# First image in another order, and the queries' weight loaded by the scalar engine's queue

## The chip, the cores and the metric

One core of one Trainium2 chip runs the kernel. The metric is the device time of one execution in microseconds, as a median over runs. The kernel before takes 1978.31 us (three runs, 1976.14 to 1979.01).

## What is computed

A self-attention block over 16 images of 512 channels and 32x32 positions, with a group norm ahead of it, four 512x512 weights and a residual, all in float32:

```python
residual = hidden_states
h = group_norm(hidden_states, norm_gamma, norm_beta)
q = conv1x1(h, wq, bq)
k = conv1x1(h, wk, bk)
v = conv1x1(h, wv, bv)
...
attn = jnp.einsum('bci,bcj->bij', qf, kf) * scale
attn = jax.nn.softmax(attn, axis=2)
out = jnp.einsum('bcj,bij->bci', vf, attn).reshape(B, C, H, W)
out = conv1x1(out, wo, bo)
return residual + out
```

## The kernel before

The program is written by hand, engine by engine: one block each for SyncE, GpSimd, TensorE, ScalarE and VectorE, with semaphores between them. What an engine does is the order of the lines of its block; nothing is scheduled for it. Image 0 is written out apart (`first=True`), the others run in a loop.

**Precision.** Every float32 factor is split in two: ScalarE makes a rounded high part (`*_hi`), VectorE subtracts it to get the rest (`*_lo`), and `product` (lines 418 to 421) makes three matmuls of them, high by high and the two mixed ones. So each factor costs a cast on ScalarE, then a subtraction on VectorE, and only then TensorE may use it.

**Setup, once.** The product of the weights of queries and keys is made first (lines 431 to 438, 48 matmuls, into banks 0 to 3); it takes the place of two of the projections. Twelve filler matmuls on zeros run ahead of it (line 428). Then `wo` is transposed by TensorE (line 444), a bias vector is summed by GpSimd and multiplied out in four one-column matmuls (lines 447 to 452), and the product of the transposed `wo` with `wv` is made (lines 453 to 462, 48 matmuls, banks 4 to 7). It waits for the low parts of `wo` (VectorE, line 989) and of `wv` (GpSimd, line 361). Meanwhile VectorE takes the group norm's statistics of image 0 (lines 895 to 933), GpSimd turns them into a scale and a shift per channel (lines 366 to 385), and ScalarE applies these to the image (`normalise`, line 642).

**The first image.** The product T of weight and image uses seven block products (a Strassen-like scheme) instead of eight. The blocks of the image are A11, A12, A22 and the sums S1 to S4, which VectorE makes (lines 945 to 957), ScalarE casts (line 651) and VectorE splits (line 964). `make_first_t` on TensorE (line 472) runs the seven products in `T_ORDER`, two halves r = 0, 1 for each, six matmuls of 512 columns a half. Three of them reuse a bank, so ScalarE copies the partial sum out before ("a", "b", "y", line 715). VectorE then adds up six blocks D3, D1, D2, B11, B22, B21 from banks and copies (`add_t`, lines 1022 to 1051), and each of these and D4 is cast (line 724) and split (`low_t`, line 1057).

**The scores.** `make_scores` (lines 516 to 555) takes the seven block products of T with the image in `S_ORDER`: product 7 for four column groups q, then product 1, and so on. Ahead of product 1 for q = 0 TensorE waits until B21 for r = 0 is added, since that addition reads the bank which product 1 overwrites:

```python
if p == 1:
    if q == 0:
        pe.wait_ge(t_split, t_count(b, first, 7, 0, L_AT[4]))
        pe.wait_ge(t_added, t_count(b, first, 6, 0, C_AT["B21"]))
```

After the scores come column maxima, exponentials, the values' product and the outputs, image by image; their code is not touched.

**Loads.** SyncE issues all loads of the start in one queue (lines 276 to 287): `wk` and `wq` in four pieces each by turns, `bq`, the image, `wo`, three vectors of 512 numbers (gamma, beta, `bo`), `wv`.

## Time and profile before

| | us |
|---|---|
| median of 3 runs | 1978.31 |
| the profiled execution | 1976.81 |
| its span, first to last instruction | 1974.8 |
| TensorE busy in the span | 1966.2 |
| VectorE busy | 1630.7 |
| ScalarE busy | 998.1 |
| GpSimd busy | 327.0 |

The mean granted clock of TensorE is 0.999 of full. Times in the rows below are counted from the start of the span. A row of the timeline begins with the start and the duration; instructions of one engine overlap by a little (the next one starts before the last has been acknowledged), so the distance from start to start is what one costs where an engine is busy throughout. In brackets stands the idle time before a row, and what ended it.

### The profile page before, as it was taken

Reading aid. Unit: us, or ns where it says so; the run is one execution under the profiler, and the core shown is the slowest. Engines: PE = TensorE matmul, PEld = TensorE weight load, DVE = VectorE, ACT = ScalarE, POOL = GpSimd, SP = SyncE. Lnnn points to the kernel's source line nnn. Section 1 sums busy time; section 2 is a strip of 40 time slices with the busy share of each in tenths; the row PEclk is TensorE's granted clock in tenths of the full one; section 3 lists DMA queues with packets and bytes.
Section 4 is the critical chain, followed back from the end, with each engine's and each line's share of the span. In section 5 each row is a group of like instructions: output and inputs, shape, how many; then the busy total and the mean of one; then the engine's idle time right before and its main releaser. Section 6 shows DMA issues by size and latency. Waiting matters only on the chain.

```text
span 1974.8 us, 29827 instructions
## 1 busy us (share of the span) xinstructions
PE 1966.2 (100%) x9924; PEld 1680.8 (85%) x9924; DVE 1630.7 (83%) x2285; ACT 998.1 (51%) x1528; POOL 327.0 (17%) x240
## 2 busy tenths in 40 slices
PE   9999999999999999999999999999999999999999
PEld 7888888888888888888888888888888888888887
DVE  8998896978969789696887969889698896978857
ACT  6474453645536464454644536446364553646443
POOL 2022120111202012020121201212011120212202
PEclk9999999999999999999999999999999999999999
DMA  7336252363414535054350533615236252363402
GB/s 250 128 150 171 76 148 96 149 170 127 114 77 155 164 149 139 31 173 146 149 159 32 173 125 149 170 66 151 102 149 170 108 124 87 150 169 149 92 31 43
DMA packets 55035, 254.66 MB, mean 129 GB/s; under 512 B 8160, under 2 KB 8160, under 8 KB 50400
## 3 DMA queue, kind: packets, MB, share of 16 engines
q1 hardware_dynamic: 36720, 221.01, 29.8%
q0 software_dynamic: 18288, 33.30, 10.8%
q8 instruction: 16, 0.26, 0.1%
q14 instruction: 11, 0.09, 0.0%
HBM read 213.39 MB, written 74.45 MB: 146 GB/s over the span
## 4 chain that ended last, share of the span: by engine, by line
PE 94%; DVE 0%; issue 0%; POOL 0%; ACT 0%; POOLq 0%
PE psum L419 32%; PE psum L420 31%; PE psum L421 31%; DVE red L1161 0%; DVE scores L1166 0%; POOL wide L394 0%; DVE scores L1152 0%; DVE scores L1351 0%; DVE scores L1220 0%; ACT room L730 0%; POOLq L393 0%; ACT scores L744 0%
## 5 line engine op out<-in xcount | busy, mean ns | idle before, releaser
L419 PE MATMUL psum<-big_hi 128*128 128x512 f32 x1056 | 412.0, 390 | 1.6 <-POOL big_lo L361 1.6
L420 PE MATMUL psum<-big_lo,big_hi 128*128 128x512 f32 x1056 | 411.6, 390 | 0.0
L421 PE MATMUL psum<-big_hi,big_lo 128*128 128x512 f32 x1056 | 411.4, 390 | 0.0
L419 PE MATMUL psum<-big_hi,h_hi 128*128 128x512 f32 x896 | 348.5, 389 | 0.0
L420 PE MATMUL psum<-big_lo,h_hi 128*128 128x512 f32 x896 | 348.5, 389 | 0.0
L421 PE MATMUL psum<-big_hi,h_lo 128*128 128x512 f32 x896 | 348.5, 389 | 0.0
L1152 DVE TENSOR_TENSOR scores<-psum,room 128x512 f32<-128x512 f32 x192 | 130.6, 689 | 199.6 <-ACT room L826 149.6
L826 ACT COPY room<-psum 128x512 f32<-128x512 f32 x192 | 113.1, 589 | 291.2 <-PE psum L421 291.2
L419 PE MATMUL psum<-w_split,h_hi 128*128 128x256 f32 x896 | 253.6, 283 | 0.3 <-ACT room L730 0.3
L420 PE MATMUL psum<-w_split,h_hi 128*128 128x256 f32 x896 | 253.6, 283 | 0.0
L421 PE MATMUL psum<-w_split,h_lo 128*128 128x256 f32 x896 | 253.6, 283 | 0.0
L419 PEld LDWEIGHTS psum<-big_hi 128*128 128x128 f32 x1056 | 198.8, 188 | 42.6 <-issue 1.7
L421 PEld LDWEIGHTS psum<-big_hi,big_lo 128*128 128x128 f32 x1056 | 198.6, 188 | 41.7
L420 PEld LDWEIGHTS psum<-big_lo,big_hi 128*128 128x128 f32 x1056 | 198.8, 188 | 40.6
L1173 DVE TENSOR_TENSOR big_lo<-scores,big_hi 128x512 fp32r<-128x512 f32 x256 | 197.2, 810 | 24.9 <-ACT big_hi L754 24.9
L420 PEld LDWEIGHTS psum<-big_lo,h_hi 128*128 128x128 f32 x896 | 168.2, 188 | 35.0
L421 PEld LDWEIGHTS psum<-big_hi,h_lo 128*128 128x128 f32 x896 | 168.2, 188 | 34.9
L419 PEld LDWEIGHTS psum<-big_hi,h_hi 128*128 128x128 f32 x896 | 168.2, 188 | 34.9
L394 POOL PARTITION_ALL_REDUCE wide<-red x32 | 56.9, 1828 | 841.2 <-DVE red L1161 841.2
L1166 DVE TENSOR_TENSOR scores<-scores,wide 128x1024 f32<-128x1024 f32 x128 | 162.8, 1322 | 32.8 <-POOL wide L394 32.8
L405 POOL PARTITION_ALL_REDUCE wide<-red x32 | 104.1, 3254 | 478.3 <-DVE red L1201 469.4
L419 PE MATMUL psum<-h_hi,w_split 128*128 128x512 f32 x448 | 174.5, 389 | 0.0
(134 smaller groups left out, 3445.3 us busy)
## 6 DMA issues: line engine op xcount, KB each, us to landing
w_split<-kept_t SPq DMA_DIRECT2D x15, 3584.0 KB, 11.8
w_split<-kept_v SPq DMA_DIRECT2D x15, 3584.0 KB, 11.3
room<-in_x SPq DMA_DIRECT2D x64, 512.0 KB, 3.5
out<-scores POOLq DMA_DIRECT2D x127, 256.0 KB, 6.8
room<-in_x SPq DMA_DIRECT2D x61, 256.0 KB, 5.7
red<-in_x SPq DMA_DIRECT2D x30, 256.0 KB, 3.7
wide<-in_x SPq DMA_DIRECT2D x30, 256.0 KB, 6.9
kept_t<-w_split SPq DMA_DIRECT2D x1, 3584.0 KB, 10.9
```

What stands on the lines that cost most here:

```text
L394: nc.gpsimd.partition_all_reduce(wide[:, half, :], red[:, half, :], P, MAX_ALL).then_inc(max_all, 1)
L405: nc.gpsimd.partition_all_reduce(wide[:, half, :], red[:, half, :], P, ADD_ALL).then_inc(sum_all, 1)
L419: nc.tensor.matmul(o, a_hi, b_hi, start=start, stop=False, skip_group_check=True)
L420: nc.tensor.matmul(o, a_hi, b_lo, start=False, stop=False, skip_group_check=True)
L421: return nc.tensor.matmul(o, a_lo, b_hi, start=False, stop=stop, skip_group_check=True)
L826: nc.scalar.copy(snap_s(q, n), bank[alpha_s[q % 2]][:]).then_inc(s_snapped, 1)
L1152: nc.vector.tensor_tensor(scores[:, o, :], bank[at][:], snap_s(q, n), ALU.add).then_inc(s_added, 1)
L1166: nc.vector.tensor_tensor(scores[:, j:j + 2, :], scores[:, j:j + 2, :], wide[:, half, :].unsqueeze(1).to_broadcast([P, 2, HALF]), ALU.subt ...
L1173: nc.vector.tensor_tensor(p_lo[:, j, :], scores[:, half * NJ + j, :], p_hi[:, j, :].bitcast(F32), ALU.subtract).then_inc(p_split, 1)
```

## The change

All of it lies in the setup and in image 0. The loads of `wq` go from SyncE's queue to ScalarE's, two before and two after the load of the table of functions; gamma, beta and `bo` go there too, gamma and beta behind the eight casts of `wk` and `wq`. On TensorE eight fillers stay of twelve; the bias matmuls go ahead of the transposes of `wo` and into another bank; the product with `wv` starts when its first pieces are split. VectorE, not GpSimd, splits the first piece of `wv`. Image 0 takes its blocks in another order (A12 and product 2 ahead of S1 and product 5), casts and splits A22 and A12 ahead of the splits of the weight, and interleaves the additions and splits of T differently. The code that all later images run is as before.

```diff
+T_FIRST = (4, 2, 5, 7, 6, 1, 3)
...
-H_FIRST = (A22, S1, A12, S3, S2, A11, S4)
+H_FIRST = (A22, A12, S1, S3, S2, A11, S4)
...
@@ sync
             for o in range(KC):
                 sp.dma_start(wk_raw[:, o, :], w_d["k"][:, o, :]).then_inc(wk_in[o], 16)
-                sp.dma_start(wq_raw[:, o, :], w_d["q"][:, o, :]).then_inc(wq_in[o], 16)
...
-            for n, a in enumerate(vec_d):
-                sp.dma_start(vecs[:, n, :], a, allow_slow_non_contiguous=True).then_inc(vec_in, 16)
@@ gpsimd
-            pool.wait_ge(vec_in, 16 * len(vec_d))
+            pool.wait_ge(scale_in, 32)
...
-            for o in range(KC):
+            for o in range(1, KC):
                 low_wv(o)
@@ tensor
-            for _ in range(12):
+            for _ in range(8):
...
             pe.wait_ge(consts_set, 4)
+            pe.wait_ge(bias_step, 2)
+            for c in range(KC):
+                mm = nc.tensor.matmul(bank[2 * KC - 1][:, c:c + 1], wide[:, 0, cols(c)], primer[:, 0:1],
+                                      start=True, stop=True, skip_group_check=True)
+            mm.then_inc(bias_summed, 1)
             for c in range(KC):
                 pe.wait_ge(wo_in[c], 16)
             for n in range(KC):
+                if n == KC - 1:
+                    pe.wait_ge(t_bias_set, 1)
...
                 if o == 0:
-                    pe.wait_ge(t_bias_set, 1)
-                pe.wait_ge(wot_split, KC if o == 0 else o + 1)
-                pe.wait_ge(wv_split, o + 1)
+                    pe.wait_ge(wv_first, 1)
+                else:
+                    pe.wait_ge(wv_split, o)
                 for c in range(KC):
+                    if o == 0:
+
+                        pe.wait_ge(wot_split, c + 1)
...
-                pe.wait_ge(wt_split, 7)
-                for p in T_ORDER:
+                pe.wait_ge(wt_split, 3)
+                for p in T_FIRST:
+                    pe.wait_ge(wt_split, W_AT[p])
@@ scalar
+            for o in range(2):
+                act.dma_start(wq_raw[:, o, :], w_d["q"][:, o, :]).then_inc(wq_in[o], 16)
             nc.scalar.preload_act_table(ACT.Exp)
+            for o in range(2, KC):
+                act.dma_start(wq_raw[:, o, :], w_d["q"][:, o, :]).then_inc(wq_in[o], 16)
...
+            for n in range(2):
+                act.dma_start(vecs[:, n, :], vec_d[n], allow_slow_non_contiguous=True).then_inc(scale_in, 16)
...
+            act.dma_start(vecs[:, 2, :], vec_d[2], allow_slow_non_contiguous=True).then_inc(vec_in, 16)
...
+            high_wot(0)
+            high_raw_wv(0)
+            for o in range(1, KC):
+                high_wot(o)
+            for o in range(1, KC):
+                high_raw_wv(o)
             for k in (2, 3):
                 normalise(0, k)
+            high_h(0, 0, True)
+            high_h(0, 1, True)
 
             act.wait_ge(wd_set, 4)
             for p in W_ORDER:
                 high_wt(p)
-            high_h(0, 0, True)
...
+                for r in range(2):
+                    snap(0, r, 0, "a", T_FIRST_AT[4], True)
                 high_h(0, 2, True)
-                high_h(0, 1, True)
                 copy_wov(0)
                 copy_wov(1)
                 high_h(0, 3, True)
-                for r in range(2):
-                    snap(0, r, 0, "a", T_AT[4], True)
@@ vector
+                if o == 0:
+                    dve.wait_ge(wv_high, 1)
+                    nc.vector.tensor_tensor(wvs_lo[:, 0, :], wv_raw[:, 0, :], wvs_hi[:, 0, :].bitcast(F32),
+                                            ALU.subtract).then_inc(wv_first, 1)
...
+            low_h(0, 0, True)
+            low_h(0, 1, True)
             for p in W_ORDER:
...
-            low_h(0, 0, True)
...
-                low_h(0, 1, True)
                 low_h(0, 2, True)
-
-                dve.wait_ge(bv_in, 16)
-                dve.wait_ge(vec_in, 16 * len(vec_d))
-                for c in (0, 1):
-                    row_dots(c)
                 low_h(0, 3, True)
                 sum_h(0, 2, True)
 
+                dve.wait_ge(bv_in, 16)
+                dve.wait_ge(vec_in, 16)
+                row_dots(0)
+                low_h(0, 4, True)
+                low_h(0, 5, True)
+                row_dots(1)
...
-                low_h(0, 6, True)
-                low_t(0, 0, "D3", True)
-                low_t(0, 1, "D3", True)
-                for name in C_ORDER[1:]:
-                    for r in range(2):
-                        add_t(0, r, name, True)
-                for name in L_ORDER[1:]:
-                    for r in range(2):
-                        low_t(0, r, name, True)
...
+                low_both("D3")
+                add_both("D1", "D2", "B11")
+                low_both("D4", "B11", "D2", "D1")
+                add_both("B22", "B21")
+                low_both("B22", "B21")
```

On VectorE, from the last split of a block of the image to the end of the splits of T (L964 is `low_h`, L1037 to L1050 are the additions D1, D2, B11, B22, B21, L1057 is `low_t`), before:

```order
L1057 TENSOR_TENSOR big_lo<-scores,big_hi 128x512 [waits t_high] x2
L1037 TENSOR_TENSOR scores<-psum,scores 128x512 [waits t_snapped,t_summed]
L1037 TENSOR_TENSOR scores<-psum,room 128x512 [waits t_snapped,t_summed]
L1041 SCALAR_TENSOR_TENSOR scores<-psum,t_bias,scores 128x512 [waits t_snapped,t_summed]
L1041 SCALAR_TENSOR_TENSOR scores<-psum,t_bias,room 128x512 [waits t_snapped,t_summed]
L1044 TENSOR_TENSOR scores<-scores 128x512 [waits t_added] x2
L1046 TENSOR_TENSOR scores<-scores 128x512 [waits t_added] x2
L1050 TENSOR_TENSOR scores<-psum,scores 128x512 [waits t_high] x2
L1057 TENSOR_TENSOR big_lo<-psum,big_hi 128x512 [waits t_high] x2
L1057 TENSOR_TENSOR big_lo<-scores,big_hi 128x512 [waits t_high] x10
L1234 TENSOR_TENSOR scores<-wide 128x512 [waits wov_copied,t_split]
```

And with the change, at the same place (L986 is `low_h`, L1062 to L1077 the additions, L1084 `low_t`):

```order
L1084 TENSOR_TENSOR big_lo<-scores,big_hi 128x512 [waits t_high] x2
L1064 TENSOR_TENSOR scores<-psum,scores 128x512 [waits t_snapped,t_summed]
L1064 TENSOR_TENSOR scores<-psum,room 128x512 [waits t_snapped,t_summed]
L1068 SCALAR_TENSOR_TENSOR scores<-psum,t_bias,scores 128x512 [waits t_snapped,t_summed]
L1068 SCALAR_TENSOR_TENSOR scores<-psum,t_bias,room 128x512 [waits t_snapped,t_summed]
L1071 TENSOR_TENSOR scores<-scores 128x512 [waits t_added] x2
L1084 TENSOR_TENSOR big_lo<-psum,big_hi 128x512 [waits t_high] x2
L1084 TENSOR_TENSOR big_lo<-scores,big_hi 128x512 [waits t_high] x6
L1073 TENSOR_TENSOR scores<-scores 128x512 [waits t_added] x2
L1077 TENSOR_TENSOR scores<-psum,scores 128x512 [waits t_high] x2
L1084 TENSOR_TENSOR big_lo<-scores,big_hi 128x512 [waits t_high] x4
```

The additions of B22 and B21 (L1073, L1077) now stand behind eight splits (L1084 x2 and x6) that stood behind them before.

On ScalarE, from the bias terms to the casts of the weight, before (L671 casts `wo`, L674 `wv`, L642 is `normalise`, L658 casts the weight, L651 a block of the image):

```order
L674 CAST big_hi<-scores 128x512 [waits wv_in3]
L642 ACTIVATE room<-room,h_shift,h_scale 128x1024 [waits scale_step] x2
L658 ACTIVATE w_split<-psum 128x512 [waits wkq_summed,wd_set]
L658 ACTIVATE w_split<-psum 128x512 [waits wkq_summed] x2
L658 ACTIVATE w_split<-scores 128x512 [waits wd_set] x4
L651 CAST h_hi<-room 128x1024 [waits h_full]
L642 ACTIVATE room<-room,h_shift,h_scale 128x1024 [waits scale_step] x2
L651 CAST h_hi<-room 128x1024 [waits h_full,bias_summed]
L651 CAST h_hi<-scores 128x1024 [waits h_summed]
L693 COPY wide<-psum 128x512 [waits wov_summed] x2
L651 CAST h_hi<-scores 128x1024 [waits h_summed]
```

With the change (L673 and L679 load the vectors, L688 casts `wo`, L692 `wv`, L653 is `normalise`, L669 casts the weight, L662 a block):

```order
L692 CAST big_hi<-scores 128x512 [waits wv_in3]
L653 ACTIVATE room<-room,h_shift,h_scale 128x1024 [waits scale_step] x2
L662 CAST h_hi<-room 128x1024 [waits h_full] x2
L669 ACTIVATE w_split<-psum 128x512 [waits wkq_summed,wd_set]
L669 ACTIVATE w_split<-psum 128x512 [waits wkq_summed] x2
L669 ACTIVATE w_split<-scores 128x512 [waits wd_set] x4
L653 ACTIVATE room<-room,h_shift,h_scale 128x1024 [waits scale_step] x2
L738 COPY scores<-psum 128x512 [waits t_summed,bias_summed]
L738 COPY room<-psum 128x512 [waits h_split,h_summed,t_summed]
L662 CAST h_hi<-red 128x1024 [waits h_summed]
L716 COPY wide<-psum 128x512 [waits wov_summed] x2
L662 CAST h_hi<-scores 128x1024 [waits h_summed]
```

Two loads stand ahead of the bias terms and one behind them, and the casts of two blocks stand ahead of those of the weight.

On TensorE, behind the first product of weights, before:

```order
L421 MATMUL psum<-big_hi,big_lo 128x512
L444 MATMUL psum<-ident,scores 128x128 [waits wo_in2,wo_in1,wo_in3,wo_in0,consts_set]
L444 MATMUL psum<-ident,scores 128x128 x15
L450 MATMUL psum<-primer,wide 128x1 [waits bias_step,wot_split]
L450 MATMUL psum<-primer,wide 128x1 x3
L419 MATMUL psum<-big_hi 128x512 [waits wv_split,wot_split,t_bias_set]
```

With the change (L444 is the bias, L453 the transpose, L420 opens the product with `wv`):

```order
L422 MATMUL psum<-big_hi,big_lo 128x512
L444 MATMUL psum<-primer,wide 128x1 [waits bias_step,consts_set]
L444 MATMUL psum<-primer,wide 128x1 x3
L453 MATMUL psum<-ident,scores 128x128 [waits wo_in2,wo_in3,wo_in1,wo_in0]
L453 MATMUL psum<-ident,scores 128x128 x11
L453 MATMUL psum<-ident,scores 128x128 [waits t_bias_set]
L453 MATMUL psum<-ident,scores 128x128 x3
L420 MATMUL psum<-big_hi 128x512 [waits wot_split,wv_first]
```

The bias matmuls, and with them the wait for GpSimd's sum (`bias_step`), have come ahead of the transposes.

## Rows read from the trace of the kernel before

**Rows 1.** The page, part 1: busy time, share of the span, instructions by engine.

```profile
PE 1966.2 (100%) x9924; PEld 1680.8 (85%) x9924; DVE 1630.7 (83%) x2285; ACT 998.1 (51%) x1528; POOL 327.0 (17%) x240
```

**Rows 2.** Timeline of TensorE, from the fillers to the first scores: start, duration, line.

```profile
1.58 5.49 PE L429 MATMUL psum<-h_hi 128*128 128x512 f32 x12 [1.58 <-DVE h_hi L967]
...
6.87 0.62 PE L419 MATMUL psum<-big_hi 128*128 128x512 f32 x1
...
19.06 1.94 PE L444 MATMUL psum<-ident,scores 128*128 128x128 f32 x16 [0.88 <-DMA scores<-in_wo]
...
23.79 0.47 PE L419 MATMUL psum<-big_hi 128*128 128x512 f32 x1 [1.65 <-POOL big_lo L361]
...
28.20 0.40 PE L419 MATMUL psum<-big_hi 128*128 128x512 f32 x1
...
36.38 0.39 PE L419 MATMUL psum<-h_hi,w_split 128*128 128x512 f32 x1
...
55.42 0.39 PE L419 MATMUL psum<-big_hi,h_hi 128*128 128x512 f32 x1
...
60.87 0.39 PE L419 MATMUL psum<-big_hi,h_hi 128*128 128x512 f32 x1
```

**Rows 3.** Chain that ended last, where image 0 goes from scores to values: start, duration.

```profile
92.79 0.60 DVE scores L1152
```

**Rows 4.** Timeline of VectorE in setup and image 0.

```profile
12.05 5.15 DVE L895 BATCH_NORM_STATS2 bn<-room 128x6 f32<-128x512 f32 x8 [0.84 <-DMA room<-in_x]
...
20.34 2.48 DVE L989 TENSOR_TENSOR big_lo<-psum,big_hi 128x512 fp32r<-128x512 f32 x4 [0.15 <-ACT big_hi L671]
...
27.67 0.69 DVE L1007 SCALAR_TENSOR_TENSOR w_split<-psum,w_split 128x512 fp32r<-128x512 f32 x1 [1.51 <-ACT w_split L658]
...
48.24 1.23 DVE L964 TENSOR_TENSOR h_lo<-red,h_hi 128x1024 fp32r<-128x1024 f32 x1
...
49.39 1.29 DVE L1057 TENSOR_TENSOR big_lo<-scores,big_hi 128x512 fp32r<-128x512 f32 x2
...
55.98 1.28 DVE L1050 TENSOR_TENSOR scores<-psum,scores 128x512 f32<-128x512 f32 x2
...
58.37 6.10 DVE L1057 TENSOR_TENSOR big_lo<-scores,big_hi 128x512 fp32r<-128x512 f32 x10
...
73.08 2.50 DVE L1225 TENSOR_TENSOR w_split<-scores,w_split 128x512 fp32r<-128x512 f32 x4 [2.48 <-ACT w_split L704]
```

**Rows 5.** Timeline of SyncE's issues of loads.

```profile
1.30 0.43 SPq L278 DMA_DIRECT2D scores<-in_wq  x1
...
10.73 2.20 SPq L285 DMA_DIRECT2D vecs<-in_beta  x1
```

**Rows 6.** Stretches: busy us by engine, granted clock, DMA share, GB/s.

```profile
5.00:5.50 0.50, 0.50 (x2) 0.40 (x2) 0.50 (x1) 0.00 (x0) 0.00 (x0) 1.00 0.70 135
...
14.00:14.50 0.50, 0.50 (x4) 0.42 (x3) 0.50 (x2) 0.00 (x0) 0.50 (x1) 1.00 1.10 451
...
17.50:18.00 0.50, 0.50 (x3) 0.22 (x2) 0.45 (x5) 0.00 (x0) 0.00 (x0) 1.00 1.32 130
...
24.00:26.00 2.00, 2.00 (x7) 1.52 (x7) 1.97 (x4) 2.00 (x2) 2.00 (x2) 0.60 0.03 8
```

**Rows 7.** Timeline of GpSimd in the setup.

```profile
15.92 1.29 POOL L376 TENSOR_TENSOR wide<-wide 128x512 f32<-128x512 f32 x1
...
22.37 5.01 POOL L361 TENSOR_TENSOR big_lo<-scores,big_hi 128x512 fp32r<-128x512 f32 x4
```

**Rows 8.** Timeline of ScalarE in setup and image 0.

```profile
10.79 1.34 ACT L664 ACTIVATE red<-scores,bq_s 128x512 f32<-128x512 f32 x2 [0.30 <-DMA bq_s<-in_bq]
...
19.72 2.05 ACT L671 CAST big_hi<-psum 128x512 fp32r<-128x512 f32 x4 [2.28 <-PE psum L444]
...
23.79 2.38 ACT L642 ACTIVATE room<-room,h_shift,h_scale 128x1024 f32<-128x1024 f32 x2
...
29.59 1.07 ACT L651 CAST h_hi<-room 128x1024 fp32r<-128x1024 f32 x1
```

More of the change, by code:

```diff
@@ L32 @@
 T_AT = {p: n + 1 for n, p in enumerate(T_ORDER)}
+T_FIRST = (4, 2, 5, 7, 6, 1, 3)
+T_FIRST_AT = {p: n + 1 for n, p in enumerate(T_FIRST)}
 W_ORDER = (2, 1, 3, 4, 5, 7, 6)
@@ L647, in high_h @@
                 if a in (A11, A12, A22):
-                    act.wait_ge(h_full, 2 if first and a == A22 else count(b, KC, KC))
+                    act.wait_ge(h_full, 2 if first and a in (A22, A12) else count(b, KC, KC))
                 else:
@@ L668, in _, with high_wot, high_raw_wv @@
             nc.scalar.copy(b12_copy, b12).then_inc(b12_copied, 1)
-            for o in range(KC):
+            act.wait_ge(bias_summed, 1)
+            nc.scalar.copy(t_bias[:], bank[2 * KC - 1][:, 0:KC]).then_inc(t_bias_set, 1)
+            def high_wot(o):
                 act.wait_ge(wo_turned, o + 1)
                 nc.scalar.copy(wot_hi[:, o, :], bank[KC + o]).then_inc(wot_high, 1)
-            for o in range(KC):
+            def high_raw_wv(o):
                 act.wait_ge(wv_in[o], 16)
                 nc.scalar.copy(wvs_hi[:, o, :], wv_raw[:, o, :]).then_inc(wv_high, 1)
-                if o == 0:
-                    act.wait_ge(bias_summed, 1)
-                    nc.scalar.copy(t_bias[:], bank[KC][:, 0:KC]).then_inc(t_bias_set, 1)
+            high_wot(0)
[4 more added lines that the diff above has]
+                high_raw_wv(o)
             for k in (2, 3):
                 normalise(0, k)
+            high_h(0, 0, True)
+            high_h(0, 1, True)
             act.wait_ge(wd_set, 4)
@@ L719, in high_t @@
                 if name == "D4":
-                    act.wait_ge(t_summed, t_count(b, first, 7, r, T_AT[3]))
+                    act.wait_ge(t_summed, t_count(b, first, 7, r, (T_FIRST_AT if first else T_AT)[3]))
                     nc.scalar.copy(t_hi[:, OF_T[p], r, :], bank[alpha_t[r]][:]).then_inc(t_high, 1)
@@ L948, in sum_h @@
                     dve.wait_ge(h_full, count(b, KC, KC))
-                    nc.vector.tensor_tensor(blocks[S1], a21, blocks[A22], ALU.add).then_inc(h_summed, 1)
+                    nc.vector.tensor_tensor(blocks_[S1], a21, blocks[A22], ALU.add).then_inc(h_summed, 1)
                 elif n == 1:
@@ L953, in sum_h @@
                     dve.wait_ge(h_summed, count(b, 4, 1))
-                    nc.vector.tensor_tensor(blocks[S2], blocks[S1], blocks[A11], ALU.subtract).then_inc(h_summed, 1)
+                    nc.vector.tensor_tensor(blocks[S2], blocks_[S1], blocks[A11], ALU.subtract).then_inc(h_summed, 1)
                 else:
@@ L1029, in add_t @@
                 if name == "D3":
-                    dve.wait_ge(t_summed, t_count(b, first, 7, r, T_AT[5]))
+                    dve.wait_ge(t_summed, t_count(b, first, 7, r, (T_FIRST_AT if first else T_AT)[5]))
                     dve.wait_ge(t_snapped, t_count(b, first, 3, r, 1))
@@ L1034, in add_t @@
                 elif name == "D1":
-                    dve.wait_ge(t_summed, t_count(b, first, 7, r, T_AT[7]))
+                    dve.wait_ge(t_summed, t_count(b, first, 7, r, (T_FIRST_AT if first else T_AT)[7]))
                     dve.wait_ge(t_snapped, t_count(b, first, 3, r, 3))
@@ L1038, in add_t @@
                 elif name == "D2":
-                    dve.wait_ge(t_summed, t_count(b, first, 7, r, T_AT[1]))
+                    dve.wait_ge(t_summed, t_count(b, first, 7, r, (T_FIRST_AT if first else T_AT)[1]))
                     dve.wait_ge(t_snapped, t_count(b, first, 3, r, 2))
@@ L1086, in make_first_t, with add_both, low_both @@
                     row_dots(c)
+                low_h(0, 6, True)
                 dve.wait_ge(bv_used, KC)
                 nc.vector.tensor_tensor(out_bias[:], wo_bv[:], bo_s, ALU.add).then_inc(biases_set, 1)
-                low_h(0, 6, True)
-                low_t(0, 0, "D3", True)
-                low_t(0, 1, "D3", True)
-                for name in C_ORDER[1:]:
-                    for r in range(2):
-                        add_t(0, r, name, True)
-                for name in L_ORDER[1:]:
-                    for r in range(2):
-                        low_t(0, r, name, True)
+                def add_both(*names):
+                    for name in names:
+                        for r in range(2):
+                            add_t(0, r, name, True)
+                def low_both(*names):
+                    for name in names:
+                        for r in range(2):
+                            low_t(0, r, name, True)
+                low_both("D3")
[3 more added lines that the diff above has]
+                low_both("B22", "B21")
             def left(b, n):
```

25 lines of the change are left out of this document (9 added, 16 removed).

## The prediction

> **What bounds the kernel now.** First the page's busy times [rows 1]: TensorE works 1966.2 of 1974.8 us, so only its idle and slow stretches, 8.6 us in all, can be won, and whatever makes it wait is paid in full. The change touches the setup and image 0 alone, so the timeline of TensorE up to the first scores [rows 2] comes next. The reader is to see there three losses: the fillers and the wait up to 6.87, where the first product begins; 0.88 us ahead of the transposes at 19.06, for the load of `wo`; and 1.65 us ahead of the product with `wv` at 23.79, for GpSimd's split. That product then runs slowly at first: its opening twelve matmuls last from 23.79 to 28.20, 4.41 us, where a half of T (six matmuls) takes 1.36 (fourteen of them from 36.38 to 55.42), so 2.72 for twelve: 1.7 us lost. From 28.20 to the end of product 7 of the scores at 60.87 TensorE has no hole.
>
> Next the chain of waits [rows 3]: from 92.79 on, where image 0 goes from scores to values, it has left TensorE and runs over VectorE for a dozen us. Up to there VectorE must keep pace, or nothing that TensorE gains lasts. So the third view is VectorE's timeline [rows 4]: it is late from the statistics on (they begin at 12.05, for the image's load), it idles 1.51 us ahead of 27.67, and 2.48 ahead of 73.08, for casts that follow TensorE's scores. Its order of work, not TensorE's, is what I follow below.
>
> The sum is made against the profiled execution, 1976.81 us (span 1974.8 and 2.0 around it), which lies 1.50 below the median of the three runs, 1978.31.
>
> **The change, part by part.**
>
> *Loads of `wq`.* Eight issues of SyncE fall to four, at 0.43 us each [rows 5]. ScalarE now issues two ahead of its function table and two behind it; by the same row that is some 1.9 us before its first cast is free to start, about 4.0 instead of 3.6. No row shows an issue on ScalarE; the bounds are 0.43 and the 2.20 of SyncE's row for beta [rows 5], and I take 0.43, the row of the same load. The bytes in front of the image and of `wo` stay the same, and the 16 engines are busy with them: share 1.10 at 14 us, though only 0.70 at 5 [rows 6]. A second queue may fill such dips. The statistics would then begin sooner by the 0.84 us for which VectorE waits ahead of 12.05 [rows 4], and by what its eight splits of `wk` and `wq` ahead of that, 4.9 us of work, come sooner: about 1 us by the dip, 1.9 in all as the upper bound; the lower is 0. Against it gamma, beta and `bo`, 4-byte pieces, now run among the image and ahead of `wo`; at 17.5 us, where they run now, half a microsecond moved 130 GB/s where 451 is normal [rows 6], 0.36 us lost, so up to 0.9 for three. I take 0 for both together. The Trainium skill, DMA: Bandwidth & Descriptors, section on issuing engines that are not separate DMA queues, says that loads of several engines interleave on the same 16 DMA engines and that only issue time is saved; by it the second queue gives nothing, which is the 0 that I take, and the dip at 5 us is what speaks against it.
>
> *Fillers.* Four fewer, 5.49 / 12 x 4 = 1.8 us [rows 2]. The first product starts earlier by up to 0.9 us (its inputs come at about 6.0), but ends at the wait for `wo`, which the transposes still have until 19.06: hidden, 0. If that cover went, 0.9 would be won.
>
> *Bias matmuls ahead of the transposes.* They need GpSimd's sum, ready at 15.92 + 1.29 = 17.21 [rows 7]. Two issues of vectors on ScalarE ahead of the bias terms (10.79, [rows 8]) make this 18.1: still ahead of 19.06. Hidden, 0.
>
> *Product with `wv`.* VectorE has the first low part of `wo` at 20.34 + 0.61 and of `wv` 0.61 later [rows 4], so TensorE starts at 21.75 instead of 23.79. The other pieces wait for casts on ScalarE and GpSimd's 1.25 us each [rows 7], which keep pace. With TensorE at full clock T can begin at 32.6 instead of 36.38: 2.0 from the start and 1.7 from the clock, 3.7 us won on TensorE. Does it last?
>
> *ScalarE.* From 19.72, eight casts of 0.51 [rows 8] end at 23.8 as before; two `normalise` at 1.15 (26.1); then A22 and A12 at 0.95 each, ready at 27.2 and 28.1; the weight's seven casts to 31.5; the other two `normalise` to 33.9, one cast later than now.
>
> *VectorE.* From 20.34: five splits of 0.61 instead of four (`wv` is new), 23.4; four differences and a step, some 2.8, 26.2; a wait to 27.2; A22 and A12 at 1.15 each, 29.5; seven splits of the weight, 33.7. S1 waits for `normalise` and is summed at 35.1, S3 at 36.3. Now VectorE and ScalarE take turns. ScalarE must first copy both halves of snapshot "a", of which TensorE has the second at 35.5; so S1's cast ends at 37.1, its split at 38.3; two copies of the weight stand ahead of S3's cast (39.05; split 40.3); S2 is summed at 41.4, cast at 42.5, split at 43.7; A11 at 44.9; row product, D3, S4's sum, D3, two row products (0.6 to 0.7 each, the sum 1.15) to 49.4; S4 is split from 49.7 to 50.9. In the rows of before that ended at 48.24 + 1.23 = 49.47. VectorE has idled some 3.5 us in turns, against 2 before, and done one split more: it is 1.4 us late, and D3's split, behind `out_bias` now, starts at 51.1 instead of 49.39 [rows 4], 1.7 late.
>
> *The additions of T.* Here lies the largest term. Product 1 of the scores waits for B21 at r = 0. Now this is the second last pair of additions [rows 4]: it starts at 55.98, 6.6 us behind D3's split at 49.39, and TensorE needs it at 60.87, so there are over 4 us in hand. With the change eight splits stand ahead of it, 8 x 0.61 = 4.9 us. B21 for r = 0 comes at 51.1 + 6.6 + 4.9 + 0.1 or so: at 62.7, used at 62.85. TensorE, with holes of 0.4 (S1), 0.2 and 1.5 (S4) in T, would be ready for product 1 at 53.8 + 4 x 1.36 = 59.2. It stands still for 3.6 us and begins product 1 at 62.85 instead of 60.87: **2.0 us late**. All that was won by starting sooner is lost in these holes.
>
> *Behind it.* From there the order is as before. VectorE's 2.48 us of idle ahead of 73.08 end with a cast that follows the scores, so it shifts by 2.0 too, and so do the loads of image 1, the chain from 92.79 on, and every image.
>
> Sum: +3.7 won, -3.7 back in holes, 2.0 lost: 1976.81 + 2.0 = 1978.8 for such an execution, 1978.31 + 2.0 = **1980.3** for the median. It is +0.1%; 0.2% (4.0 us) is about what a measurement of this kernel can tell from no change. So I forecast no change that can be told, on the slow side.
>
> **Rivals.**
>
> *The clock falls in the hole before product 1* (1982.0). The granted clock read 0.60 from 24 to 26 us [rows 6], 1.2 GHz for a good part, after TensorE had idled 0.88 and 1.65 us around sixteen short transposes and a few one-column matmuls; it cost 1.7. A hole of 3.6 is longer than these. If so, +2.0 + 1.7 = +3.7, near the bound; with S4's hole or a slow start of the `wv` product too, up to 1.0 more. For: the length. Against: matmuls are dense right before it. The Trainium skill, TensorE: Matmul & The Clock Gate, section on HAM oscillation, says that idle gaps between bursts put the clock back to half and the next burst starts slow; by that rule this is the likelier case, and the row at 24 us agrees with it, but no row has a single hole among dense matmuls.
>
> *ScalarE's issues block* (slower, 1982.9). If gamma and beta take 2.20 each, as beta did on SyncE with a full queue behind the image [rows 5], the bias terms start 4.4 late, GpSimd's sum comes at 21.6, and the transposes, now behind the bias matmuls, start at 21.7 instead of 19.06. ScalarE's casts and all that hangs on them go 2.6 later: 2.0 + 2.6 = +4.6. It decides from a bias sum later than 19.0. Against: ScalarE's own queue holds only `wq` at that time.
>
> *Two queues carry more* (1978.4). If image and `wo` land 1.9 sooner, all moves by 1.9 and the loss is about 0: 2.0 - 1.9 = +0.1. For: the dip at 5 us. Against: share 1.10 later.
>
> *The turns cost nothing* (1974.3 or less). If VectorE has B21 in time after all, TensorE keeps its 3.7 to 4. It would need VectorE to be 5 us sooner than reckoned, more than all its idle time there: little chance.
>
> **How the numbers follow.** Forecast 0.47, clock 0.24, blocked issue 0.12, two queues 0.13, nothing lost 0.04. Faster by over 0.2%: the last case, 0.04. Slower: the blocked issue and 0.12 of the clock's 0.24 (half of it adds up to over 4.0): 0.24. The rest, 0.72, is within 0.2%. The unknown costs move the forecast by some 2 us either way (loads 1.9 down; 0.9 up for the vectors, 1 more for the turns). The range from 1976.9 to 1984.0 takes in the forecast, the clock and most of the other two; some 0.1 is left out at either end.
>
> **What would show it.** Right: in the profile after, TensorE starts the product with `wv` at about 21.8 and T near 33; S4 is split at about 51; the last wait ahead of product 1 of the scores is for an addition of VectorE (line 1077), some 3.6 us long; product 1 starts near 63; the wait ahead of VectorE's weight splits near 75 stays. Wrong: the bias matmuls end later than 19; the first product or the transposes end sooner by over a us; product 1 starts before 60.9; or VectorE reaches D3's splits before 49.4.

## Result, and the profile after

| | before | after |
|---|---|---|
| median, us (12 runs each) | 1978.32 | 1982.53 |
| lowest to highest | 1975.64 to 1979.01 | 1981.65 to 1985.79 |
| profiled execution | 1976.81 | 1981.65 |
| its span | 1974.8 | 1979.6 |

The ratio is 1.0025 [1.0018, 1.0032]. By the medians the change is slower by 4.2 us (by the ratio, which lies near that of the means, by 4.9): 2.2 more than forecast, inside the range and just over the 0.2% that can be told from no change. It lies next to the rival of the falling clock (1982.0). Of the kernels below, fillers12 and both_undone had one execution each that took far longer (10239.43 and 2160.86 us), which the ratios leave out and without which their medians would be 1982.05 and 1977.32.

Busy times on the page of after, to be held against [rows 1], and a queue that before did not have:

```profile
PE 1966.6 (99%) x9920; PEld 1679.0 (85%) x9920; DVE 1631.4 (82%) x2286; ACT 999.5 (50%) x1528; POOL 346.7 (18%) x239
...
q10 hardware_dynamic: 2160, 1.06, 0.2%
```

TensorE works as long as before (1966.6 against 1966.2 us) and stands idle for 13.0 us of the span instead of 8.6, so the time went into holes, stretches in which it waits. TensorE's timeline of after shows where (start, duration, line, count, and in brackets the idle time ahead and its releaser), to be held against [rows 2]:

```profile
1.58 3.78 PE L430 MATMUL psum<-h_hi 128*128 128x512 f32 x8 [1.58 <-DVE h_hi L989]
6.40 0.77 PE L420 MATMUL psum<-big_hi 128*128 128x512 f32 x1 [1.03 <-DVE big_lo L998]
...
11.12 0.40 PE L422 MATMUL psum<-big_hi,big_lo 128*128 128x512 f32 x1
...
19.55 0.94 PE L444 MATMUL psum<-primer,wide 128*128 128x1 f32 x8
20.36 1.95 PE L453 MATMUL psum<-ident,scores 128*128 128x128 f32 x16
22.99 0.50 PE L420 MATMUL psum<-big_hi 128*128 128x512 f32 x1 [0.69 <-DVE big_lo L1015]
...
34.02 0.39 PE L420 MATMUL psum<-h_hi,w_split 128*128 128x512 f32 x1
...
52.31 0.47 PE L420 MATMUL psum<-h_hi,w_split 128*128 128x512 f32 x1 [1.24 <-DVE h_lo L986]
...
64.02 0.47 PE L420 MATMUL psum<-big_hi,h_hi 128*128 128x512 f32 x1 [3.27 <-DVE scores L1077]
...
109.54 0.39 PE L420 MATMUL psum<-w_split,h_hi 128*128 128x256 f32 x1 [0.50 <-ACT room L753]
```

Read it by what each place has lost or won against before. The first product starts at 6.40 instead of 6.87, but TensorE had been idle for 1.03 us, and the product's opening eleven matmuls take 4.72 us (6.40 to 11.12, 0.43 from start to start) where eleven at the later pitch, 0.23 from start to start, take 2.5: 2.2 us lost. So the transposes begin at 20.36, 1.30 later than before. The product with `wv` begins at 22.99 (before 23.79) and T at 34.02 (before 36.38): 2.36 us ahead. Then come the hole of S4, 1.24, and that of B21, 3.27: product 1 of the scores begins at 64.02 where it was at 60.87, **3.15 us late**.

VectorE's timeline of after, against [rows 4], shows why:

```profile
11.41 5.31 DVE L917 BATCH_NORM_STATS2 bn<-room 128x6 f32<-128x512 f32 x8 [1.11 <-DMA room<-in_x]
...
21.65 0.69 DVE L1011 TENSOR_TENSOR big_lo<-psum,big_hi 128x512 fp32r<-128x512 f32 x1 [1.94 <-ACT big_hi L688]
...
50.98 1.23 DVE L986 TENSOR_TENSOR h_lo<-red,h_hi 128x1024 fp32r<-128x1024 f32 x1 [0.30 <-ACT h_hi L662]
...
52.19 1.29 DVE L1084 TENSOR_TENSOR big_lo<-scores,big_hi 128x512 fp32r<-128x512 f32 x2
...
63.19 1.29 DVE L1077 TENSOR_TENSOR scores<-psum,scores 128x512 f32<-128x512 f32 x2
...
76.95 2.50 DVE L1259 TENSOR_TENSOR w_split<-scores,w_split 128x512 fp32r<-128x512 f32 x4 [2.48 <-ACT w_split L727]
```

B21's addition (L1077) begins 11.0 us behind D3's split (52.19), before 6.6. The weight's splits near 75 keep their 2.48 us of idle, and begin at 76.95 instead of 73.08: +3.87. The span ends 4.8 us later.

### The profile page after: what moved, and what is told of

It reads as the page before. It is cut to its first block, busy times and chain, and to the rows that moved or that the text cites. A ratio compares the mean times of both kernels' runs of the same rounds, so it can differ in the third digit from the quotient of the medians.

```text
span 1979.6 us, 29819 instructions
## 1 busy us (share of the span) xinstructions
PE 1966.6 (99%) x9920; PEld 1679.0 (85%) x9920; DVE 1631.4 (82%) x2286; ACT 999.5 (50%) x1528; POOL 346.7 (18%) x239
## 4 chain that ended last, share of the span: by engine, by line
PE 94%; DVE 0%; issue 0%; POOL 0%; ACT 0%; POOLq 0%
PE psum L420 31%; PE psum L422 31%; PE psum L421 31%; DVE red L1195 0%; DVE scores L1200 0%; POOL wide L395 0%; DVE scores L1186 0%; DVE scores L1385 0%; DVE scores L1254 0%; ACT room L753 0%; POOLq L394 0%; ACT scores L767 0%
## 5 line engine op out<-in xcount | busy, mean ns | idle before, releaser
L420 PE MATMUL psum<-big_hi 128*128 128x512 f32 x1056 | 412.2, 390 | 1.7 <-DVE big_lo L998 1.0
L420 PE MATMUL psum<-big_hi,h_hi 128*128 128x512 f32 x896 | 348.7, 389 | 3.6 <-DVE scores L1077 3.3
L420 PE MATMUL psum<-w_split,h_hi 128*128 128x256 f32 x896 | 253.6, 283 | 0.5 <-ACT room L753 0.5
L420 PEld LDWEIGHTS psum<-big_hi 128*128 128x128 f32 x1056 | 198.8, 188 | 43.5 <-DVE big_lo L995 1.7
L420 PEld LDWEIGHTS psum<-big_hi,h_hi 128*128 128x128 f32 x896 | 168.2, 188 | 39.3 <-issue 3.7
L420 PE MATMUL psum<-h_hi,w_split 128*128 128x512 f32 x448 | 175.4, 391 | 1.5 <-DVE h_lo L986 1.5
```

The source lines that it names most:

```text
L420: nc.tensor.matmul(o, a_hi, b_hi, start=start, stop=False, skip_group_check=True)
```

## Experiments

They were made in three steps. The kernel before ran beside each on the same chip.

### The parts, undone one by one

**fillers12.** The changed kernel with twelve fillers, so that TensorE is busy up to its first inputs.

```diff
-            for _ in range(8):
+            for _ in range(12):
```

> The changed kernel with twelve fillers again. Theory A (fillers and clock): in the changed kernel TensorE stood idle from 5.36 to 6.40 and then ran its first matmuls at half speed, so that the first product ended at 19.5 and held up the transposes, while wo had landed by 18.3. With twelve fillers the first product starts near 6.9 at full speed and ends near 18, the transposes start near 18.5 instead of 20.36, and the time falls by 1.5 to 2.2 us, to about 1980.6. Rival B (the load on the scalar queue itself is what costs, by later casts): the first product ends no sooner or the transposes still start near 20, and the time stays within 0.5 us of 1982.5.

Measured: 1982.14, ratio 1.0021 [1.0012, 1.0030], against 1977.87 before. Its profiled execution is the lowest of its runs, 1979.98; there product 1 begins at 62.34 instead of 64.02, behind a hole of the same 3.27 us. So in that trace the start was worth 1.7 us, but the median stayed within 0.4 of the changed kernel's, where 1.5 to 2.2 less was expected. Something else costs two microseconds in most executions and is not in this trace.

**adds_first.** The changed kernel with every addition of T ahead of the splits, as before the change.

```diff
-                add_both("D1", "D2", "B11")
-                low_both("D4", "B11", "D2", "D1")
-                add_both("B22", "B21")
-                low_both("B22", "B21")
+                add_both("D1", "D2", "B11", "B22", "B21")
+                low_both("D4", "B11", "D2", "D1", "B22", "B21")
```

> The changed kernel with all additions of T ahead of the splits, as before the change. Theory A (order of the additions): the wait ahead of product 1 of the scores is then for the splits of B11, some 2 us sooner (62.0 instead of 64.02), and the wait for the snapshot at 67.3 goes: 2.0 to 2.6 us less, about 1980.0. Rival C (VectorE is late by its turns with ScalarE, the order of the additions only moves the wait): product 1 starts within 0.5 us of 64.0 and the time stays near 1982.5.

Measured: 1978.11, ratio 1.0002 [0.9993, 1.0010]. This one edit takes back all that the change cost: 0.24 us above its own runs of before (1977.87), where the changed kernel was 4.2 above. TensorE's timeline of adds_first: 

```profile
61.67 0.50 PE L420 MATMUL psum<-big_hi,h_hi 128*128 128x512 f32 x1 [1.33 <-DVE big_lo L1084]
```

The hole is 1.33 instead of 3.27, and product 1 is 2.35 sooner than in after. The time gained, 4.0, is 1.6 us more than this, and more than the 2.0 to 2.6 expected. It is so although this trace, too, has the first product at half pitch (from 6.24 to 10.22 us): the step from 3.27 to 1.33 us of hole is worth more than its length.

**both_undone.** Twelve fillers and the additions first.

> Twelve fillers and all additions ahead of the splits. If theory A holds in both parts they add up: product 1 of the scores starts near 60.2, 1978.0 to 1978.5, no different from the kernel before. If the two are one and the same slack, the gain is that of the larger one alone, about 1980.

Measured: 1977.49, ratio 0.9999 [0.9990, 1.0008]. Product 1 begins at 60.23, 0.6 ahead of before, and nothing of it is left at 105.61, where TensorE waits for ScalarE's snapshot (its copy of a partial sum out of a bank) as it did at 105.43 in before.

**reordered.** Twelve fillers; B21 added ahead of B22, and the splits of D2 and D1 behind both, so that only four splits stand ahead of B21; three weight casts of ScalarE put behind the first snapshots.

```diff
...
-            for _ in range(8):
+            for _ in range(12):
...
-                low_both("D4", "B11", "D2", "D1")
-                add_both("B22", "B21")
-                low_both("B22", "B21")
+                low_both("D4", "B11")
+                add_both("B21", "B22")
+                low_both("D2", "D1", "B22", "B21")
```

> Twelve fillers; behind D3's splits the additions D1, D2, B11, the splits of D4 and B11, then B21 and B22, then the other splits; ScalarE casts three pieces of the second weight behind the first two snapshots of the scores. Theory A: B21 at r = 0 is added about 13 instructions behind D3's first split instead of 18, at about 58.5, so product 1 of the scores starts near 58.7, 2 us sooner than in the kernel before, and the time is about 1976.2. Rival C: the stretch from 69 to 75 us is bound by VectorE and eats the gain; then 1978 or more.

Measured: 1977.35, ratio 0.9998 [0.9989, 1.0007], between the two theories. Product 1 begins at 58.76, as expected, with no wait ahead of it, but a wait of 0.90 us for ScalarE's snapshot follows at 62.56 and one of 0.89 for VectorE at 97.23. What TensorE gains ahead of the scores is given back where VectorE sets the pace, as [rows 3] let one expect; in this trace VectorE itself had waited 1.81 us, ahead of 81.73, for a load of image 1.

### The change's halves

**load_alone.** The kernel before with the four loads of `wq` on ScalarE's queue, nothing else.

```diff
-                sp.dma_start(wq_raw[:, o, :], w_d["q"][:, o, :]).then_inc(wq_in[o], 16)
...
+            for o in range(2):
+                act.dma_start(wq_raw[:, o, :], w_d["q"][:, o, :]).then_inc(wq_in[o], 16)
             nc.scalar.preload_act_table(ACT.Exp)
+            for o in range(2, KC):
+                act.dma_start(wq_raw[:, o, :], w_d["q"][:, o, :]).then_inc(wq_in[o], 16)
```

> The kernel before with nothing but the loads of wq moved to the scalar engine's queue (twelve fillers, vectors on SyncE's queue, old order). Theory D (two queues fill the dips): the weights land 1 to 1.5 us sooner, the image and wo some 0.5, the product with wv starts some 0.5 sooner than 23.79; 1977.4 to 1978.2. By rival B (the load on the scalar queue costs): casts and statistics later, 1979 or more. By the rule that the second queue only saves issue time: 1978.3, landings as before.

Measured: 1978.01 against 1977.75, ratio 1.0005 [0.9996, 1.0014]. The loads alone are worth nothing that can be told. The product with `wv` begins at 23.21 in its trace, 0.58 sooner than in before, but that is not the second queue's doing: fillers8_timed below, with all these loads on SyncE, has it at 22.91.

**order_alone.** The changed kernel with `wq` back on SyncE.

> The changed kernel with the loads of wq back on SyncE's queue by turns with wk; eight fillers and the new order stay. Theory A (the gap behind the eight fillers starves the clock): the first product's inputs come at about 5.6, TensorE idles only 0.2 us, the product begins near 5.6 and ends near 18, the transposes wait for wo until 19, product 1 of the scores starts near 62.8 as forecast: 1980.5 to 1981.2. If the clock falls all the same, the first product ends at 18 to 19 and the time is 1981 to 1982.5. Rival B: faster than the changed kernel by what the load cost, 1980 or less.

Measured: 1982.27, ratio 1.0025 [1.0016, 1.0035], the whole loss, where 1980.5 to 1981.2 was expected if the start is on time. It is on time here: the first product begins at 5.77, behind 0.41 us of idle, and runs at full pitch from 6.75. Its profiled execution (1982.76) shows what those of after and fillers12 do not. TensorE's timeline of order_alone:

```profile
62.34 0.77 PE L421 MATMUL psum<-big_hi,h_hi 128*128 128x512 f32 x1 [3.28 <-DVE scores L1074]
62.90 0.63 PE L422 MATMUL psum<-big_lo,h_hi 128*128 128x512 f32 x1
...
67.60 0.63 PE L421 MATMUL psum<-big_hi,h_hi 128*128 128x512 f32 x1
68.02 0.47 PE L422 MATMUL psum<-big_lo,h_hi 128*128 128x512 f32 x1
68.33 0.39 PE L423 MATMUL psum<-big_hi,h_lo 128*128 128x512 f32 x1
```

and its stretches (from:to, length, busy time of PE, PEld, DVE, ACT, POOL with counts, granted clock, DMA share, GB/s):

```profile
60.00:62.00 2.00, 0.00 (x0) 0.00 (x0) 2.00 (x4) 0.97 (x2) 0.00 (x0) 0.84 0.00 0
62.00:64.00 2.00, 1.66 (x4) 1.40 (x5) 2.00 (x5) 2.00 (x5) 0.00 (x0) 0.50 0.00 0
64.00:66.00 2.00, 2.00 (x6) 1.52 (x6) 1.93 (x4) 1.59 (x3) 0.00 (x0) 0.50 0.00 0
66.00:68.00 2.00, 2.00 (x6) 1.54 (x5) 1.97 (x4) 0.16 (x1) 0.00 (x0) 0.50 0.00 0
68.00:70.00 2.00, 2.00 (x10) 1.63 (x9) 1.79 (x3) 0.97 (x2) 0.00 (x0) 0.96 0.00 0
```

Product 1 begins at 62.34 as in fillers12, but at 1.2 GHz: the granted clock fell inside the hole, with TensorE idle for 3.28 us, and came back at about 68 us. The thirteen matmuls from 62.34 to 68.02 take 5.68 us instead of 3.0. At the wait for the snapshot before the values TensorE is at 111.19, where fillers12 was at 107.98: 2.7 us of this are the slow matmuls, and the rest comes with a wait for VectorE (0.79 us at 102.38) that fillers12 does not have.

**fillers8_before.** The kernel before with eight fillers in place of twelve, one execution.

> The kernel before with eight fillers instead of twelve. Looked at for TensorE's first product: with theory A the fillers end at 5.4, the product starts at about 5.6, and the trace shows whether its matmuls run at 0.227 or 0.43 us from start to start and until when. The time should not move by more than 0.5 us, since the transposes wait for wo until 19.06.

Measured: 1974.98. Fewer fillers did no harm there: the first product came at 5.83 at full pitch.

### The clock, by itself

One trace shows that the clock can fall in the hole, not how often. So the hole was filled with work of no use.

**hole_filled.** fillers12 and thirteen more matmuls ahead of product 1, into a bank whose last reader is done.

```diff
                     if p == 1:
                         if q == 0:
+                            if first:
+                                pe.wait_ge(t_added, t_count(b, first, 6, 1, C_AT["D2"]))
+                                for _ in range(13):
+                                    nc.tensor.matmul(bank[5], h_hi[:, 0, 0, 0:P], h_hi[:, 0, 0, :], start=True,
+                                                     stop=True, skip_group_check=True)
```

> The changed kernel with twelve fillers at the start (as in fillers12: median 1982.14, its profiled execution 1979.98) and 13 further products of no use in the hole ahead of product 1 of the scores of the first image, into bank 5, behind the addition of D2 r=1 that reads that bank last. Their results are overwritten, nothing else changes, and B21 still comes when it came, so the hole before is busy and no shorter. Theory of the clock (the hole of 3.3 us lets the granted clock fall in most executions, as the trace of order_alone shows with 0.50 from 62 to 68 us): the median falls to about 1980.0, the value of the execution of fillers12 whose clock did not fall, and the spread narrows. Theory that only the hole's length counts: the same 1982.1 as fillers12.

Measured: 1980.23 (1979.12 to 1981.31), ratio 1.0016 [1.0007, 1.0025], against 1982.14 for fillers12. TensorE's timeline of hole_filled:

```profile
58.83 3.11 PE L542 MATMUL psum<-h_hi 128*128 128x512 f32 x13
62.30 0.47 PE L420 MATMUL psum<-big_hi,h_hi 128*128 128x512 f32 x1 [0.36 <-DVE scores L1082]
...
65.59 0.47 PE L420 MATMUL psum<-big_hi,h_hi 128*128 128x512 f32 x1 [0.32 <-ACT room L853]
...
100.37 0.39 PE L420 MATMUL psum<-w_split,h_hi 128*128 128x256 f32 x1 [1.00 <-DVE scores L1191]
```

Product 1 begins no sooner, 62.30 against 62.34, and still the median is 1.9 us lower (1.5 if each is held against before on its own chip). The two intervals overlap, so the times alone would not settle it; the clocks below do.

**hole_filled_8.** The same thirteen in the changed kernel itself, with its eight fillers.

> The changed kernel (eight fillers at the start) with the same 13 products in the hole ahead of product 1. Profiled execution of the changed kernel 1981.65, median 1982.53. Theory of the clock: if its other executions are slower by a fall in that hole, the median comes down to the profiled 1981.6 or below; theory that its loss at the start (first product at half pitch, 1.3 to 2 us) and the hole are all: no change, 1982.5.

Measured: 1979.58 (1979.20 to 1982.17), ratio 1.0014 [1.0005, 1.0023]: 2.95 us less than the changed kernel, 2.1 if each is held against its own runs of before (1977.43 and 1978.32). The mean granted clock that is recorded with each execution says the same. It was 1.000 in all 22 executions of these two kernels, but in 2 of 12 of after, in 1 of 10 of fillers12 and in none of 9 of order_alone (the rest 0.999 or less). In adds_first and both_undone, where the hole lasts 1.33 and 1.32 us, it was 1.000 in 10 of 11 each. A stretch as in order_alone takes 3.4 us of full clock out of 1980.7, 0.17%, which is its recorded 0.998; the 0.999 of nine executions of after stands for a shorter one. Two things limit this figure. It does not count the start: the record of the clock in a trace begins with the clock's first rise (at 10.96 us in after), and what lies ahead of that is taken as 1.00. And it counts the end: in the trace of fillers12 (0.999) the only fall is at 1975.80, behind the start of the last matmul at 1973.42. So a single 0.999 says little, but 22 of 22 against 3 of 31 says that the clock fell in the hole. The profiled execution of after is one of its two with 1.000, and its lowest: the fall that most of its executions have is not on its page. It has the slow start instead, which hole_filled_8's trace does not have (there, too, 0.95 us of idle stood ahead of the first product, and the first matmul took 0.47).

**fillers8_timed.** The kernel before with eight fillers again, timed.

> The kernel before with eight fillers in place of twelve, timed (one execution gave 1974.98). Theory that fewer fillers cost by themselves: 1979 to 1980. Theory that the fillers matter only where the load of the weights comes late, and that the executions of the kernel before are spread by the clock at the product with wv: 1978 as before, spread from 1975 to 1979.

Measured: 1977.23 (1975.58 to 1978.59), ratio 0.9999 [0.9990, 1.0008]. The number of fillers costs nothing by itself; the 1974.98 above was an execution in which the product with `wv` ran at full clock, which it did not in this one's trace.

**wv_filled.** The kernel before has a hole of 1.65 us ahead of the product with `wv`, with a granted clock of 0.60 behind it [rows 2, 6]. Six matmuls of no use fill it.

```diff
                     pe.wait_ge(t_bias_set, 1)
+                    pe.wait_ge(wot_split, 2)
+                    for _ in range(6):
+                        nc.tensor.matmul(bank[KC + 1], h_hi[:, 0, 0, 0:P], h_hi[:, 0, 0, :], start=True,
+                                         stop=True, skip_group_check=True)
```

> The kernel before with six products of no use, into bank 5, between the sum of the bias and the product with wv (the hole of 1.65 us on GpSimd's split; behind it 9 or so matmuls start 0.43 us apart instead of 0.23, at a granted clock of 0.60 and 0.54). Theory that the hole lets the clock fall in most executions: 1.5 to 2 us faster than before, 1976.0 to 1976.4. Theory that the fall comes of something earlier: same as before, 1977.8 to 1978.3.

Measured: 1976.18 (1975.29 to 1977.61) against 1977.43, ratio 0.9996 [0.9987, 1.0005]. TensorE's timeline of wv_filled, then its stretches (PE alone: length, busy time, clock, DMA share, GB/s):

```profile
22.00 1.66 PE L458 MATMUL psum<-h_hi 128*128 128x512 f32 x6 [0.26 <-ACT t_bias L681]
23.50 0.39 PE L419 MATMUL psum<-big_hi 128*128 128x512 f32 x1
```

```profile
24.00:26.00 2.00, 2.00 (x11) 1.00 0.04 8
26.00:28.00 2.00, 2.00 (x10) 1.00 0.00 0
```

The product begins at 23.50 instead of 23.79 and now at 1.00 where [rows 6] had 0.60.

**wv_filled_again.** The same kernel on another chip.

> The same kernel as wv_filled once more, on whatever chip comes: there its median was 1.25 us under that of the kernel before (1976.18 against 1977.43), with an interval of the ratio that still held 1. Theory that the fall of the clock behind the hole ahead of the product with wv is in most executions of the kernel before and gone here: 1 to 2 us faster again. Theory that the difference was chance: within 0.5 us of the kernel before.

Measured: 1976.16 against 1977.88, ratio 0.9992 [0.9983, 1.0001]. Twice 1.3 to 1.7 us less, each time with an interval that just holds 1. It is the lowest median of all kernels here. Its clock was recorded as 1.000 in 21 of 22 executions, that of the kernel before, beside these two, in 10 of 48: the clocks show that the fall is gone, the times alone do not show a gain.

## Why the prediction was right and wrong

**Right: the hole.** The largest term was B21 behind eight more splits, a hole of 3.6 us ahead of product 1 and a loss of 2.0. The trace has 3.27, for L1077 as named; S4 is split at 50.98 and D3 at 52.19, later than the 49.7 and 51.1 reckoned, by the slow start. Where the start is on time (fillers12, order_alone) they are split at 49.30 and 50.52, and product 1 begins at 62.34, 0.5 ahead of the forecast. That the order of the additions is the cause is shown by adds_first, which undoes it alone and takes back the whole loss. With the hole busy, the changed kernel takes 1979.58 and fillers12 1980.23, 2.2 and 2.8 above before: the forecast was 2.0, 1980.3. The gain of 3.7 on TensorE came as reckoned: where the start is on time the product with `wv` begins at 21.33 (order_alone; predicted 21.75), at full clock, T begins at 32.35 (predicted 32.6), and the holes eat what it wins.

**The step that failed: the choice between the forecast and the rival of the clock.** I gave a clock that stays up 0.47 and one that falls 0.24, with the argument that "matmuls are dense right before it". Dense matmuls ahead of a hole did not keep the clock. In the trace of order_alone it fell within a single hole of 3.28 us, and in most executions of after it was below 1.000. Filling the hole took 1.5 us off with twelve fillers and 2.1 with eight, each held against its own runs of before (1.0 and 2.2 by the ratios); the rival had said 1.7. The forecast left this term at 0; with it, 2.0 + 1.7 makes the rival's 1982.0. The rule that idle gaps between bursts put the clock back to half (the Trainium skill, TensorE: Matmul & The Clock Gate, section on HAM oscillation) is borne out by the 0.50 from 62 to 68 us. The row that bore most on it, 0.60 behind 1.65 us of idle [rows 6], I priced as a gain and weighed too little as a warning.

**The second step: fillers, "hidden, 0".** The first product did start earlier (6.40 against 6.87), but by less than the 0.9 allowed, since its inputs came later than the 6.0 reckoned. ScalarE's first cast, before and after:

```profile
3.59 0.62 ACT L637 CAST big_hi<-scores 128x512 fp32r<-128x512 f32 x1 [1.45 <-DMA scores<-in_wk]
```

```profile
4.31 0.62 ACT L648 CAST big_hi<-scores 128x512 fp32r<-128x512 f32 x1 [1.24 <-DMA scores<-in_wk]
```

It starts between 4.07 and 4.31 in all eight traces with the loads of `wq` on ScalarE (4.18 in load_alone, where nothing else is changed), between 3.38 and 3.62 in the six with them on SyncE. So the move delays the first inputs by 0.5 to 0.9 us, and with eight fillers TensorE idled for 1.03 us ahead of the product; order_alone, the same kernel with `wq` on SyncE, idled for 0.41. And the cover I named was not there in that execution. The first product ran at half pitch to 11.12 and became the last to be waited for: it ended at 19.5, and the bias matmuls and transposes behind it moved from 19.06 to 20.36. So one sign of being wrong did come, bias matmuls that end later than 19, but not by the rival that it was to show: GpSimd's sum was ready at 15.24 + 1.29 = 16.53, and the first product was what they waited for. Against 62.85 + 1.3 = 64.15, product 1 came at 64.02, but that agreement is luck: against the 62.34 of an on-time start the slow one cost 1.7. For the median this counts little: filling the hole gave the same time, within 0.7 us, with eight fillers and with twelve.

**Loads of `wq`, taken as 0: right for the sum.** ScalarE's rows of after, against the bounds of 0.43 and 2.20:

```profile
0.86 0.89 ACTq L642 DMA_DIRECT2D scores<-in_wq  x2
...
8.53 0.39 ACTq L673 DMA_DIRECT2D vecs<-in_gamma  x1
...
8.96 0.69 ACTq L673 DMA_DIRECT2D vecs<-in_beta  x1
...
10.11 0.73 ACT L677 ACTIVATE red<-scores,bq_s 128x512 f32<-128x512 f32 x1 [0.61 <-DMA bq_s<-in_bq]
```

0.45 for a piece of `wq`, 0.39 and 0.69 for a vector: the rival of blocked issues falls, and the bias terms start at 10.11, sooner than before. (The 0.9 us that the prediction sets against three vectors does not follow from its 0.36 for one, three times which is 1.1; it moved a bound only.) The stretch at 5 us, against 135 GB/s in [rows 6]:

```profile
5.00:5.50 0.50, 0.37 (x1) 0.00 (x0) 0.50 (x1) 0.45 (x1) 0.00 (x0) 1.00 1.08 414
```

The dip is not there, but neither is it in every trace of the old loads: fillers8_timed has 340 GB/s in this stretch with one queue. Over 2 to 8 us the eight traces with `wq` on ScalarE have 339 to 347 GB/s, the six with it on SyncE 276 to 323. Little that is waited for came sooner by it. The statistics begin at 11.41 instead of 12.05, within my bounds of 0 and 1.9, but they begin between 11.32 and 11.56 in the eight traces and between 11.17 and 12.05 in the six, so the 0.64 is not shown to be the second queue's; the first inputs came later. The rule that several issuing engines share the same DMA engines, and gain only issue time (the Trainium skill, DMA: Bandwidth & Descriptors, section on issuing engines that are not separate DMA queues), gave the right time, 0; the somewhat higher rate can be that issue time, which no run here sets apart.

**Behind product 1: "shifts by 2.0 too"** was too simple. From product 1 to the wait that was at 105.43 in before, the delay grows from 3.15 to 4.11 us in after, from 1.47 to 2.55 in fillers12 and from 1.43 to 3.75 in hole_filled. A wait of some 0.3 us for ScalarE's snapshot, which has B21's cast and three weight casts ahead of it (at 65.59 in hole_filled), is new in all three and belongs to the change. The 1.00 for VectorE at 100.37 in hole_filled does not: after and fillers12 have no such wait, and wv_filled_again, with the first image in its old order, has one of 0.64 at 96.08. In hole_filled VectorE had waited 1.41 us, ahead of 85.50, for a load of image 1. From 109 us to the end after takes 0.7 us more than before takes from 105.43; but this last part lasts between 1869.2 and 1871.0 us over the fourteen traces, so 0.7 is no more than executions differ by.

**What stays open.** Why the first product runs at half pitch in the traces of after and adds_first, behind 1.03 and 0.88 us of idle, and not in that of hole_filled_8 behind 0.95; with twelve fillers none of eight traces has it beyond 7.56 us. How many other executions have it: four of the eleven of hole_filled_8 lie at 1981.33 to 1982.17, some 2 us above most of the others, all with a clock of 1.000, which a slow start would fit, but no trace shows it. How much of the loss is the clock's, within the 1.0 to 2.2 us above. And why the clock stays up in a few executions of one kernel and falls in the others.

## What to carry to other kernels

A wait of a few microseconds on TensorE has two prices, its length and the slow matmuls behind it: price the second wherever the profile already shows one hole with a lowered clock behind it, and test it by filling the hole with matmuls of no use. Starting an engine sooner is worth nothing if another engine's order of work sets the next meeting point: follow the additions that free a bank before moving splits ahead of them. And when a change's cost hangs on the clock, one profiled execution, above all the lowest, can be the one that doesn't show it: look at the mean clock of every execution, and remember that it leaves out the start.

## What the hardware showed that was not expected

A granted clock that reads 1.00 does not mean full pitch at the start: from 6.40 to 11.12 us after's matmuls follow each other at 0.43 us, as in order_alone at 0.50, while the stretches there read 1.00. The record of the clock in that trace has its first entry at 10.96 us, and a stretch ahead of the first entry is shown as 1.00; in the fourteen traces it comes between 4.62 and 10.96 us, and where the product is already running then, its full pitch begins with it. Thirteen matmuls whose results are thrown away made fillers12 some 1.5 us faster without the product behind them starting any sooner (62.30 against 62.34 in the traces). And a second issuing engine raised the rate of the first loads (339 to 347 GB/s from 2 to 8 us, 276 to 323 with one), delayed the first cast by 0.5 to 0.9 us, and changed the time by nothing that could be told.
